# Graph attention on one core: the turns of the probabilities one by one between the output products of the chunk before

## The chip, the cores and the metric

One core of a Trainium2 chip. The metric is device time in microseconds from the kernel's start to its end; lower is better.

## The reference, cut to what matters

The kernel runs four layers one after the other on 1250 rows of 512 numbers: a graph attention, a gated feed-forward, a graph mean with a feed-forward, and a self-attention with a mixture of experts. The change is in the first:

```python
q = (x @ Wq + bq).reshape(n, H, OUT_DIM)      # n = 1250, H = 4, OUT_DIM = 512
k = (x @ Wk + bk).reshape(n, H, OUT_DIM)
v = (x @ Wv + bv).reshape(n, H, OUT_DIM)
alpha = jnp.einsum('ehc,ehc->eh', q[dst], k[src]) / np.sqrt(OUT_DIM)
amax = jax.ops.segment_max(alpha, dst, num_segments=n)
ex = jnp.exp(alpha - amax[dst])
denom = jax.ops.segment_sum(ex, dst, num_segments=n)
attn = ex / denom[dst]
agg = jax.ops.segment_sum(attn[:, :, None] * v[src], dst, num_segments=n).reshape(n, HC)
x_attn = agg + x @ Wskip + bskip
x_lin = x_attn @ Wlin + blin
...
```

## The kernel before

The attention over 21250 edges is computed densely: a matrix of edge counts, 1250 by 1250, is made in advance, and each head then computes all scores, masks those without an edge, and weights the exponentials by the counts. Products of weights that follow each other (Wq with Wk, Wv with Wlin) are folded in advance: `m` stands for the first and `g` for the second.

Each of the 4 heads has 5 chunks of 250 destination rows, and a chunk has two tiles of 125 rows (`s` is 0 or 1). All products of this layer are in three passes: each operand is kept as a rounded high half and a low half, and high by high, high by low, low by high are accumulated (`three_pass`, L127). So what leaves PSUM is evicted twice: ACT rounds it to the high half, then DVE subtracts that from the same bank to give the low half, and signals the bank as free.

For a chunk, PE does in this order:

- four `t_units`: the chunk's rows times `m`, 12 matmuls of 250 columns each, into two banks in turn (`unit`, banks 6 and 7), evicted to `t_hi`, `t_lo`;
- `y_unit(0)` of the chunk before (30 matmuls of 250 columns: probabilities times rows), then `scores(0)`, `y_unit(1)`, `y_unit(2)`, `scores(1)`, `y_unit(3)`. Units of y use the same two banks and are evicted to `yt_hi` and `yt_lo` (L1108 on ACT, L1188 on DVE);
- `turn(0)`: the ten pieces of the probabilities `prob` of tile 0, 125 by 125 each, are transposed on PE into three banks, in pieces of 4, 4 and 2 (`PIECES`), each piece with a signal `tp_done`; they are evicted to `pt_hi` (L1131 on ACT) and `pt_lo` (L1234 on DVE, `turn_lo`), which frees the piece's bank (`tp_free`);
- `out_units`: for each tile of the chunk before, 12 matmuls of 512 columns of `yt` by `g`, into the two unit banks again. A wait on `pp_free` ahead of them asks that all four y units are evicted. DVE adds each to `acc` (`add_out`, L1242);
- `turn(1)`: the same for tile 1.

While PE does so, DVE takes the maximum of a tile's scores, ACT the exponential, and DVE multiplies by the counts with the sum, and scales (`normalise_sum`, whose last step, L1228, signals `p_ready`). DVE's queue at a chunk's end is: the y unit's low half, `normalise_sum(1)`, `turn_lo(0)`, at the last chunk of a head the split of the next head's matrix (`split_lo`, L1172, behind ACT's L1102, which itself stands behind ACT's part of tile 0's turns), `add_out` twice, `turn_lo(1)`, and then the next chunk's t units. All queues are in program order and all waits are on semaphores, with values counted (`Tick`).

The first chunk of the first head has no chunk before it (`before is None`) and puts products of the skip path in these places. The outputs of the last chunk come at the end, from `last_outputs`, with no turns. In the last head DVE also normalises finished chunks.

Of the kernel before, what the change touches and what calls it, by code (L numbers as in the profile page):

```python
# [23 lines left out]
P = 125  # L24
NT = N // P
CH = 2 * P
NC = N // CH
KT = D // 128
# [64 lines left out]
class Core:  # L93
# [12 lines left out]
    def at(self, name, shape, dtype, kb):  # L106

        return self.nc.alloc_sbuf_tensor_at(name, shape, dtype, offset=self.bottom + int(kb * 1024))

    def sem(self, name):  # L110

        if name in self.credits:
            return self.credits[name]
        self.parts.append(self.nc.alloc_semaphore(name=name))
        return self.parts[-1]
# [7 lines left out]
    def bank(self, b):  # L123
        return self.psum[:, b, :]


def three_pass(nc, out, lhs, rhs, start, stop):  # L127

    (lh, ll), (rh, rl) = lhs, rhs
    nc.tensor.matmul(out, lh, rh, start=start, stop=False)  # L130
    nc.tensor.matmul(out, lh, rl, start=False, stop=False)  # L131
    return nc.tensor.matmul(out, ll, rh, start=False, stop=stop)  # L132
# [806 lines left out]
def graph_attention(core, g, w):  # L939
# [5 lines left out]
    nc, at, sem = core.nc, core.at, core.sem  # L945
# [3 lines left out]
    g_hi, g_lo = at("vl_hi", [128, KT, D], F32R, 128), at("vl_lo", [128, KT, D], F32R, 136)  # L949
# [7 lines left out]
    yt_hi, yt_lo = at("yt_hi", [128, KT, CH], F32R, 144), at("yt_lo", [128, KT, CH], F32R, 148)  # L957
    pt_hi, pt_lo = at("pt_hi", [P, NT, CH], F32R, R + 8), at("pt_lo", [P, NT, CH], F32R, R + 18)
    prob = at("prob", [P, 2, N], F32, R + 28)
# [7 lines left out]
    pp_done, pp_free, pp_hi = sem("pp_done"), sem("pp_free"), sem("pp_hi")  # L967
    s_done, s_free, m_ready, e_ready = sem("s_done"), sem("s_free"), sem("m_ready"), sem("e_ready")
    p_ready, tcol_ready = sem("p_ready"), sem("tcol_ready")
    tcol = at("t_col", [128, KT], F32, g.small + .5)  # L970
    tp_done, tp_hi, tp_free = sem("tp_done"), sem("tp_hi"), sem("tp_free")
# [10 lines left out]
    PIECES = [(0, 4), (4, 8), (8, 10)]  # L982
# [3 lines left out]
    def skip_bank(t):  # L986
        return core.bank(3 + t % 3)[0:P, :]

    def piece(q):
        j0, j1 = PIECES[q]  # L990
        return core.bank(3 + q)[0:P, 0:(j1 - j0) * P].rearrange("p (j n) -> p j n", n=P)

    def pipeline(eng, chunk, last_outputs, counts):

        chunk(0, 0, None)
        for h in range(HEADS - 1):
            chunk(h, 1, 0)  # L1000
            with eng.Fori(2, NC - 1) as c:
                for tick, per in counts:
                    tick.enter(c - 2, per)
                chunk(h, c, c - 1)
                for tick, per in counts:
                    tick.leave(NC - 3)
            chunk(h, NC - 1, NC - 2)
            chunk(h + 1, 0, NC - 1)
        for c in range(1, NC):
            chunk(HEADS - 1, c, c - 1)  # L1010
        last_outputs()

    with nc.Block() as block:
# [152 lines left out]
        def _(dve):  # L1166
# [17 lines left out]
            def unit_lo(dst_hi, dst_lo, n=D, bias=None):  # L1184
                _, b = unit()
                dve.wait_ge(pp_hi, hi.step())
                if bias is None:
                    ins = nc.vector.tensor_tensor(dst_lo, b[:, 0:n], f32(dst_hi), ALU.subtract)  # L1188
                else:
                    ins = nc.vector.scalar_tensor_tensor(dst_lo, b[:, 0:n], bias, f32(dst_hi), ALU.add, ALU.subtract)  # L1190
                ins.then_inc(pp_free, 1)
# [129 lines left out]
        @block.tensor  # L1321
        def _(pe):
            pp, tp, sub = Tick(), Tick(), Tick()

            def unit():
                v = pp.step()
                pe.wait_ge(pp_free, v)
                return bank(pp.n - 1)

            def skip(t):  # L1330
                if t >= 3:
                    pe.wait_ge(skip_added, t - 2)
                for k in range(KT):
                    pe.wait_ge(gs_lo, k + 1)
                    last = three_pass(nc, skip_bank(t), [a[:, k, t * P:(t + 1) * P] for a in (g.xt_hi, g.xt_lo)],
                                      [a[:, k, :] for a in (g_hi, g_lo)], k == 0, k == KT - 1)
                last.then_inc(skip_done, 1)

            def t_units(c):
                for m in range(KT):  # L1340
                    out = unit()
                    for k in range(KT):
                        last = three_pass(nc, out[:, 0:CH], [x[:, k, m * 128:(m + 1) * 128] for x in (m_hi, m_lo)],
                                          [x[:, k, bass.ds(CH * c, CH)] for x in (g.xt_hi, g.xt_lo)],
                                          k == 0, k == KT - 1)
                    last.then_inc(pp_done, 1)

            def scores(s, t_end):
                if s == 0:
                    pe.wait_ge(pp_free, t_end + 2)  # L1350
                pe.wait_ge(s_free, sub.step())
                for a, b in SPANS:
                    for k in range(KT):
                        last = three_pass(nc, score[:, a:b], [x[:, k, s * P:(s + 1) * P] for x in (t_hi, t_lo)],
                                          [x[:, k, a:b] for x in (g.xt_hi, g.xt_lo)], k == 0, k == KT - 1)
                last.then_inc(s_done, 1)

            def turn(s):
                v = tp.step()
                pe.wait_ge(p_ready, v)  # L1360
                pe.wait_ge(tp_free, 3 * v)
                for q, (j0, j1) in enumerate(PIECES):
                    for j in range(j0, j1):
                        last = nc.tensor.transpose(piece(q)[:, j - j0, :], prob[:, s, j * P:(j + 1) * P],
                                                   g.ident[0:P, 0:P])
                    last.then_inc(tp_done, 1)

            def y_unit(m):
                if m == 0:
                    pe.wait_ge(tp_free, 3 * (tp.base + tp.n) + 3)  # L1370
                out = unit()
                for j in range(NT):
                    last = three_pass(nc, out[:, 0:CH], [x[:, j, m * 128:(m + 1) * 128] for x in (g.xn_hi, g.xn_lo)],
                                      [x[:, j, :] for x in (pt_hi, pt_lo)], j == 0, j == NT - 1)
                last.then_inc(pp_done, 1)

            def out_units():
                pe.wait_ge(pp_free, pp.base + pp.n + 2)
                for s in range(2):
                    out = unit()  # L1380
                    for k in range(KT):
                        last = three_pass(nc, out[0:P, :], [x[:, k, s * P:(s + 1) * P] for x in (yt_hi, yt_lo)],
                                          [x[:, k, :] for x in (g_hi, g_lo)], k == 0, k == KT - 1)
                    last.then_inc(pp_done, 1)

            def chunk(h, c, before):
                def y(m):
                    if before is not None:
                        y_unit(m)
                    else:  # L1390
                        skip(AHEAD + m)

                if before is None:
                    for t in range(AHEAD):
                        skip(t)
                if isinstance(c, int) and c == 0:
                    pe.wait_ge(raw_free, 2 * h + 1)
                t_units(c)
                t_end = pp.base + pp.n
                y(0)  # L1400
                scores(0, t_end)
                y(1), y(2)
                scores(1, t_end)
                y(3)
                if before is None:
                    pe.wait_ge(skip_added, NT)
                turn(0)
                if before is not None:

                    pe.wait_ge(raw_free, 2 * h + (0 if isinstance(c, int) and c == 0 else 2))  # L1410
                    out_units()
                turn(1)

            def last_outputs():
                for m in range(KT):
                    y_unit(m)
                out_units()

            pipeline(pe, chunk, last_outputs, ((pp, 10), (tp, 2), (sub, 2)))


# [1682 lines left out]
```

## Time and profile before

| what | value |
|---|---|
| median of 3 runs | 2220.4 us (2218.78 to 2223.68) |
| span of the profiled execution | 2220.5 us; no other time is given for this execution |
| PE busy, matmuls | 2059.9 us, 93% |
| DVE busy | 1323.4 us, 60% |
| ACT busy | 836.3 us, 38% |
| POOL busy | 360.1 us, 16% |
| mean granted clock of PE | 0.969 |
| graph attention, the changed stage | from about 415 to 1229 us |

Engines: PE is TensorE's matmul, PEld its weight load, DVE VectorE, ACT ScalarE, POOL GpSimd. A row of the timeline gives start, duration, engine, line, operation, output and inputs; equal instructions that follow each other are merged, and then the duration reaches from the first one's start to the last one's end. Matmuls are pipelined, so a matmul's duration is longer than its distance to the next. In square brackets stands how long the engine was idle before, and what ended that. A granted clock of 1.00 is TensorE's full 2.4 GHz.

### The profile page before, as it was taken

Reading aid. Unit: us, or ns where it says so; the run is one execution under the profiler, and the core shown is the slowest. Engines: PE = TensorE matmul, PEld = TensorE weight load, DVE = VectorE, ACT = ScalarE, POOL = GpSimd, SP = SyncE. Lnnn points to the kernel's source line nnn. Section 1 sums busy time; section 2 is a strip of 40 time slices with the busy share of each in tenths; the row PEclk is TensorE's granted clock in tenths of the full one; section 3 lists DMA queues with packets and bytes.
Section 4 is the critical chain, followed back from the end, with each engine's and each line's share of the span. In section 5 each row is a group of like instructions: output and inputs, shape, how many; then the busy total and the mean of one; then the engine's idle time right before and its main releaser. Section 6 shows DMA issues by size and latency. Waiting matters only on the chain. (4 is left out here: it accounts for less than half of the span.)

```text
span 2220.5 us, 36706 instructions
## 1 busy us (share of the span) xinstructions
PE 2059.9 (93%) x13310; PEld 1806.2 (81%) x13310; DVE 1323.4 (60%) x2952; ACT 836.3 (38%) x1586; POOL 360.1 (16%) x308
## 2 busy tenths in 40 slices
PE   7998998999999999999999689999998999999586
PEld 5776667899999999999988569989878888888475
DVE  4574784443453454453678645556557878878766
ACT  3663993221221122122221312333336555555421
POOL 1000111000000000000000101111314453554243
PEclk9998999999999999999999889999998999999798
DMA  8760003122121211130101220201421021120542
GB/s 263 225 192 2 23 23 94 50 75 64 37 84 36 64 66 55 41 83 18 48 34 37 97 86 1 96 19 38 151 72 27 20 56 28 28 56 9 170 151 97
DMA packets 79516, 156.34 MB, mean 70 GB/s; under 512 B 7429, under 2 KB 22338, under 8 KB 77854
## 3 DMA queue, kind: packets, MB, share of 16 engines
q1 hardware_dynamic: 69802, 134.63, 20.1%
q0 software_dynamic: 4960, 11.49, 1.6%
q10 hardware_dynamic: 4616, 8.40, 1.1%
q8 instruction: 84, 1.38, 0.3%
q14 instruction: 54, 0.44, 0.1%
HBM read 104.17 MB, written 50.32 MB: 70 GB/s over the span
## 5 line engine op out<-in xcount | busy, mean ns | idle before, releaser
L130 PE MATMUL psum<-pt_hi,xn_hi 125*128 125x250 f32 x800 | 225.0, 281 | 3.3 <-DVE yt_lo L1188 1.6
L131 PE MATMUL psum<-pt_lo,xn_hi 125*128 125x250 f32 x800 | 223.8, 280 | 0.0
L132 PE MATMUL psum<-pt_hi,xn_lo 125*128 125x250 f32 x800 | 222.8, 278 | 0.0
L2412 POOL TENSOR_TENSOR mprob<-mprob,mrden 125x1250 f32<-125x1250 f32 x80 | 181.7, 2272 | 229.9 <-DVE mrden L2518 229.4
L1122 ACT ACTIVATE prob<-prob,nb 125x1250 f32<-125x1250 f32 x40 | 53.7, 1342 | 346.0 <-DVE nb L1215 346.0
L131 PE MATMUL psum<-xt_lo,t_hi 128*125 128x512 f32 (+1 forms) x480 | 170.1, 354 | 0.0
L132 PE MATMUL psum<-xt_hi,t_lo 128*125 128x512 f32 (+1 forms) x480 | 169.8, 354 | 0.0
L130 PE MATMUL psum<-xt_hi,t_hi 128*125 128x512 f32 (+1 forms) x480 | 169.1, 352 | 0.0
L2441 ACT ACTIVATE mprob<-psum,mbias 125x1250 f32<-125x1250 f32 x80 | 104.3, 1304 | 157.7 <-DVE mbias L2527 157.7
L130 PEld LDWEIGHTS psum<-pt_hi,xn_hi 125*128 125x128 f32 x800 | 151.2, 189 | 3.9 <-DVE yt_lo L1188 2.0
L2525 DVE TENSOR_REDUCE mmin<-psum 125x1 f32<-125x512 f32 (+1 forms) x240 | 127.1, 584 | 44.4 <-PE psum L2684 44.1
L131 PEld LDWEIGHTS psum<-pt_lo,xn_hi 125*128 125x128 f32 x800 | 152.1, 190 | 0.0
L132 PEld LDWEIGHTS psum<-pt_hi,xn_lo 125*128 125x128 f32 x800 | 151.8, 190 | 0.0
L704 PE MATMUL psum<-hot_src,hot_dst 125*125 125x512 bf16 (+1 forms) x624 | 131.8, 343 | 12.4 <-DVE hot_src L670 10.3
L2702 PE MATMUL psum<-ident,mprob 125*125 125x125 f32 x800 | 117.8, 292 | 21.7 <-DVE ptm_lo L2532 14.2
L2702 PEld LDWEIGHTS psum<-ident,mprob 125*125 125x125 f32 x800 | 100.1, 191 | 39.1 <-DVE ptm_lo L2532 24.8
L670 DVE TENSOR_SCALAR hot_src<-node_ids,src_f 125x1250 bf16<-125x1250 f16 x208 | 112.3, 555 | 32.3 <-PE psum L705 21.3
L2532 DVE TENSOR_TENSOR ptm_lo<-psum,ptm_hi 125x500 fp32r<-125x500 f32 (+1 forms) x240 | 126.4, 582 | 1.9 <-ACT ptm_hi L2447 1.9
L130 PE MATMUL psum<-ptm_hi,v_hi 125*128 125x250 f32 x400 | 114.8, 287 | 4.4 <-DVE ctx_lo L2538 4.4
L1209 DVE MEMSET mxc<- 125x1 f32 x40 | 2.4, 59 | 192.7 <-PE psum L132 192.7
L2684 PE MATMUL psum<-k_stack,q_chunk 128*125 128x512 f32 (+1 forms) x480 | 114.4, 375 | 2.9 <-PEq L120 2.9
L1089 POOL TENSOR_TENSOR fin_row<-fin_row 125x512 f32<-125x512 f32 x1 | 1.3, 1280 | 710.3 <-DMA gamma<-in_gamma 710.3
(503 smaller groups left out, 5854.7 us busy)
## 6 DMA issues: line engine op xcount, KB each, us to landing
slots_in<-slots_blank SPq DMA_DIRECT2D x12, 1282.5 KB, 9.2
cnt<-edge_counts SPq DMA_DIRECT2D x40, 305.2 KB
q_chunk<-q_store SPq DMA_DIRECT2D x40, 250.0 KB, 6.1
edge_attr<-in_attr SPq DMA_DIRECT2D x4, 1204.0 KB
slots_in<-slots_blank SPq DMA_DIRECT2D x3, 1539.0 KB, 16.0
moe_xg<-slots_in SPq DMA_DIRECT2D x17, 256.5 KB
raw_WvT<-in_WvT SPq DMA_DIRECT2D x4, 1024.0 KB, 6.0
raw_WskipT<-in_WskipT SPq DMA_DIRECT2D x4, 1024.0 KB, 11.8
```

The costliest lines, as they stand in the source:

```text
L130: nc.tensor.matmul(out, lh, rh, start=start, stop=False)
L131: nc.tensor.matmul(out, lh, rl, start=False, stop=False)
L132: return nc.tensor.matmul(out, ll, rh, start=False, stop=stop)
L670: nc.vector.tensor_scalar(hot_src[:, a, :], g.node_ids[0:P, :], g.src_f[:, bass.ds(GROUP * j + a, 1)], None, ALU.is_equal).then_inc(ready, 1)
L704: nc.tensor.matmul(acc[:, a:b], hot_dst[:, s, 0:P], hot_src[:, s, a:b], start=first, stop=False)
L1122: nc.scalar.activation(prob[:, s, :], prob[:, s, :], ACT.Exp, bias=nb[:, s:s + 1], scale=scale).then_inc(e_ready, 1)
L2412: nc.gpsimd.tensor_tensor(prob[:, n % 4, :], prob[:, n % 4, :], rden[:, n % 4:n % 4 + 1].broadcast_to([P, N]), ALU.mult).then_inc(p_ready, 1)
L2441: nc.scalar.activation(prob[:, n % 4, :], score[:, 0:N], ACT.Exp, bias=bias[:, n % 4:n % 4 + 1], scale=-1.0, accum_out=den[:, n % 4:n % 4 ...
L2525: last = nc.vector.tensor_reduce(low[:, s, q:q + 1], score[:, a:b], AX.X, ALU.min)
L2532: nc.vector.tensor_tensor(pt_part(n, 1, j0, j1), piece(q), f32(pt_part(n, 0, j0, j1)), ALU.subtract).then_inc(tp_free, 1)
L2684: last = nc.tensor.matmul(score[:, a:b], qs[:, half, n // 2, cols], g.k_stack[:, n // 2, a:b], start=half == 0, stop=half == 1)
L2702: last = nc.tensor.transpose(piece(q)[:, j - j0, :], prob[:, n % 4, j * P:(j + 1) * P], g.ident[0:P, 0:P])
```

## The change

The ten turns of a tile no longer form a block of their own. A new function, `out_units_and_turns`, issues the 12 matmuls of an output unit and puts one turn behind each of the second to the eleventh. Tile 0's turns go between the products of the first output unit, tile 1's between those of the second. The wait for the tile's probabilities (`turn_ready`) stands behind the unit's first product. The wait for free banks is split: each piece waits for its own bank (`turn_one`), where before a turn began when all three were free. The order of the three passes within a product group stays. The wait on `pp_free` for the evicted y units stands at the head of the new function, so it is now ahead of all turns. The first chunk keeps its turns in blocks, and the other engines' programs are as they were.

```diff
--- before.py
+++ after.py
@@ -1355,15 +1355,22 @@
                                           [x[:, k, a:b] for x in (g.xt_hi, g.xt_lo)], k == 0, k == KT - 1)
                 last.then_inc(s_done, 1)
 
+            def turn_one(s, j):
+                q = next(i for i, (j0, j1) in enumerate(PIECES) if j0 <= j < j1)
+                j0, j1 = PIECES[q]
+                if j == j0:
+                    pe.wait_ge(tp_free, 3 * (tp.base + tp.n - 1) + q + 1)
+                last = nc.tensor.transpose(piece(q)[:, j - j0, :], prob[:, s, j * P:(j + 1) * P], g.ident[0:P, 0:P])
+                if j == j1 - 1:
+                    last.then_inc(tp_done, 1)
+
+            def turn_ready():
+                pe.wait_ge(p_ready, tp.step())
+
             def turn(s):
-                v = tp.step()
-                pe.wait_ge(p_ready, v)
-                pe.wait_ge(tp_free, 3 * v)
-                for q, (j0, j1) in enumerate(PIECES):
-                    for j in range(j0, j1):
-                        last = nc.tensor.transpose(piece(q)[:, j - j0, :], prob[:, s, j * P:(j + 1) * P],
-                                                   g.ident[0:P, 0:P])
-                    last.then_inc(tp_done, 1)
+                turn_ready()
+                for j in range(NT):
+                    turn_one(s, j)
 
             def y_unit(m):
                 if m == 0:
@@ -1382,6 +1389,24 @@
                         last = three_pass(nc, out[0:P, :], [x[:, k, s * P:(s + 1) * P] for x in (yt_hi, yt_lo)],
                                           [x[:, k, :] for x in (g_hi, g_lo)], k == 0, k == KT - 1)
                     last.then_inc(pp_done, 1)
+
+            def out_units_and_turns():
+                pe.wait_ge(pp_free, pp.base + pp.n + 2)
+                for s in range(2):
+                    out = unit()
+                    for k in range(KT):
+                        cols = slice(s * P, (s + 1) * P)
+                        passes = ((yt_hi, g_hi), (yt_hi, g_lo), (yt_lo, g_hi))
+                        for i, (left, right) in enumerate(passes):
+                            n = 3 * k + i
+                            last = nc.tensor.matmul(out[0:P, :], left[:, k, cols], right[:, k, :], start=n == 0,
+                                                    stop=n == 3 * KT - 1)
+                            if n == 3 * KT - 1:
+                                last.then_inc(pp_done, 1)
+                            if n == 0:
+                                turn_ready()
+                            if 1 <= n <= NT:
+                                turn_one(s, n - 1)
 
             def chunk(h, c, before):
                 def y(m):
@@ -1404,12 +1429,12 @@
                 y(3)
                 if before is None:
                     pe.wait_ge(skip_added, NT)
-                turn(0)
-                if before is not None:
-
+                if before is None:
+                    turn(0)
+                    turn(1)
+                else:
                     pe.wait_ge(raw_free, 2 * h + (0 if isinstance(c, int) and c == 0 else 2))
-                    out_units()
-                turn(1)
+                    out_units_and_turns()
 
             def last_outputs():
                 for m in range(KT):
```

## Rows read from the trace of the kernel before

**Rows 1.** Busy time by stage: us, PE, PEld, DVE, ACT, POOL busy, PEclk, DMA.
```profile
414.00:1229.00 815.00, 806.84 (x5529) 737.76 (x5528) 408.02 (x925) 181.91 (x319) 13.60 (x6) 1.00 0.16 52
1229.00:2220.50 991.50, 885.23 (x5874) 789.59 (x5874) 669.05 (x1636) 415.43 (x816) 311.22 (x239) 0.95 0.23 67
```

**Rows 2.** PE's grouped lines, 414 to 1229: busy, mean ns, idle before, releaser.
```profile
L130 PE MATMUL psum<-vl_hi,yt_hi 128*125 128x512 f32 x160 | 65.0, 406 | 0.9 <-DVE yt_lo L1188 0.9
...
L1364 PE MATMUL psum<-ident,prob 125*125 125x125 f32 x380 | 47.8, 273 | 1.1 <-DVE pt_lo L1234 1.1
```

**Rows 3.** Timeline of PE in one chunk: start us, us, engine, line, operation.
```profile
611.73 0.28 PE L132 MATMUL psum<-pt_hi,xn_lo 125*128 125x250 f32 x1
...
612.08 0.27 PE L132 MATMUL psum<-pt_hi,xn_lo 125*128 125x250 f32 x1
612.19 1.25 PE L1364 MATMUL psum<-ident,prob 125*125 125x125 f32 x10
613.32 0.47 PE L130 MATMUL psum<-vl_hi,yt_hi 128*125 128x512 f32 x1
613.62 0.39 PE L131 MATMUL psum<-vl_lo,yt_hi 128*125 128x512 f32 x1
...
618.75 0.40 PE L132 MATMUL psum<-vl_hi,yt_lo 128*125 128x512 f32 x1
618.98 1.25 PE L1364 MATMUL psum<-ident,prob 125*125 125x125 f32 x10
...
620.19 0.28 PE L131 MATMUL psum<-xt_lo,qk_hi 128*128 128x250 f32 x1
```

**Rows 4.** Timeline of DVE in the same chunk.
```profile
612.80 0.42 DVE L1188 TENSOR_TENSOR yt_lo<-psum,yt_hi 128x250 fp32r<-128x250 f32 x1 [1.83 <-ACT yt_hi L1108]
...
615.20 0.87 DVE L1228 TENSOR_SCALAR prob<-prob,rden 125x1250 f32<-125x1250 f32 x1
615.99 1.58 DVE L1234 TENSOR_TENSOR pt_lo<-psum,pt_hi 125x500 fp32r<-125x500 f32 x3
...
619.18 0.69 DVE L1242 TENSOR_TENSOR acc<-acc,psum 125x512 f32<-125x512 f32 x1 [1.02 <-PE psum L132]
```

**Rows 5.** Timeline of PE behind the last chunk.
```profile
1219.99 0.27 PE L132 MATMUL psum<-pt_hi,xn_lo 125*128 125x250 f32 x1
1221.18 0.49 PE L130 MATMUL psum<-vl_hi,yt_hi 128*125 128x512 f32 x1 [0.92 <-DVE yt_lo L1188]
```

**Rows 6.** Timeline of PE's weight loads behind the second block of turns.
```profile
619.97 0.19 PEld L130 LDWEIGHTS psum<-xt_hi,qk_hi 128*128 128x128 f32 x1
620.08 0.19 PEld L131 LDWEIGHTS psum<-xt_lo,qk_hi 128*128 128x128 f32 x1
```

**Rows 7.** Timelines of PE, ACT and DVE at a change of head.
```profile
571.76 0.39 PE L131 MATMUL psum<-vl_lo,yt_hi 128*125 128x512 f32 x1
...
577.12 1.25 PE L1364 MATMUL psum<-ident,prob 125*125 125x125 f32 x10
578.65 0.35 PE L130 MATMUL psum<-xt_hi,qk_hi 128*128 128x250 f32 x1 [0.28 <-DVE acc L1242]
...
572.17 1.93 ACT L1102 ACTIVATE qk_hi<-raw 128x2048 fp32r<-128x2048 f32 x1
...
575.63 2.28 DVE L1172 TENSOR_TENSOR qk_lo<-raw,qk_hi 128x2048 fp32r<-128x2048 f32 x1
577.83 1.28 DVE L1242 TENSOR_TENSOR acc<-acc,psum 125x512 f32<-125x512 f32 x2
...
580.90 0.48 DVE L1190 SCALAR_TENSOR_TENSOR t_lo<-psum,t_cols,t_hi 128x250 fp32r<-128x250 f32 x1 [0.30 <-ACT t_hi L1110]
```

**Rows 8.** Timelines of DVE and PE in the last two chunks.
```profile
1154.19 2.84 DVE L1228 TENSOR_SCALAR prob<-prob,rden 125x1250 f32<-125x1250 f32 x1
...
1158.68 1.32 PE L1364 MATMUL psum<-ident,prob 125*125 125x125 f32 x10 [0.55 <-DVE pt_lo L1234]
...
1203.77 0.38 PE L130 MATMUL psum<-pt_hi,xn_hi 125*128 125x250 f32 x1 [1.65 <-DVE pt_lo L1234]
```

## The prediction

> **What bounds the kernel now.** I read the page's shares first: PE is busy for 93% of the span (the table above), too coarse to place an edit. The busy times by stage come next: from 414 to 1229 us, where the graph attention runs, PE is busy for 806.84 of 815.00 us at a granted clock of 1.00, its full 2.4 GHz [rows 1]. So in this stage the end is set by what PE's queue holds plus every gap in it, one for one. The grouped lines of the stage put 0.9 us of idle time in all ahead of the output products and 1.1 us ahead of the turns [rows 2]. DVE is busy for half of it (408 us), ACT for 182: both matter only where PE waits for them.
>
> Then one chunk of the timeline, PE alone [rows 3]. A matmul is best timed from start to start. Output products: second at 613.62, last (22 later) at 618.75: 0.233 us each. Turns: ten in 1.25 us of which the last takes 0.27, so 0.109 each. Matmuls of 250 columns: three steps from 611.73 to 612.08, 0.117 each. The reader is to see what stands at 612.19: the ten turns of tile 0, exactly between the last y product and the first output product. And at that moment [rows 4] ACT has rounded the last y unit, and DVE makes its low half from 612.80 for 0.42 us, to 613.22; the first output product, whose operand that is, starts at 613.32. **The ten turns lie in the shadow of an eviction.** They end at 613.28, just as the operand comes.
>
> The same wait without turns in front of it stands in the trace once: the outputs after the last chunk. Last y product 1219.99, first output product 1221.18, and PE idle 0.92 us for yt_lo [rows 5]. That is 1.19 us from start to start, where 612.08 to 613.32 is 1.24 with ten turns inside.
>
> **The change, part by part.** Nothing is added or taken from PE's work: 24 output products and 20 turns a chunk, as before, in 19 chunks (380 turns [rows 2]; the first chunk keeps its blocks). No DMA is moved. What moves is turn(0): it goes behind the wait for pp_free, which stays at the head of the outputs.
>
> 1. *The lost cover.* yt_lo comes from the y product's end, by an ACT and a DVE instruction that the change doesn't touch, so the second output product stays at 613.62. Behind it now come 22 further products and 20 turns instead of 22 and 10. Last output product: 613.62 + 22 x 0.233 + 20 x 0.109 = 620.93; the second t product then at 621.28, against 620.19 [rows 3]: +1.09 us, which is ten turns. In 18 chunks 19.6 us; the last chunk is summed under 5.
>
> 2. *A turn between two products.* What a turn costs there no row shows whole, but both of its seams do. Product then turn: 618.75 to 618.98, 0.23, a plain product's step. Turn then product of another kind: the last turn starts at about 619.96, the second matmul behind it at 620.19, so 0.23 for the two steps, 0.11 + 0.12. The loads tell why: the load for the matmul behind a turn starts with that turn (619.97), and the next load starts 0.11 later (620.08) [rows 6]; one load is ahead, never two. So a product covers the turn's load, as it may be hoped, but a turn is too short to cover the product's. I take 0.109, as in a block. Ends: no less than 0.057 (125 columns at a product's 512 in 0.233), which gives back 380 x 0.052 = 19.8 us; at most 0.11 more at each seam, 380 x 0.11 = 42 us, if passing between the two kinds drained PE as 613.32 to 613.62 might be read (I put that 0.30 down to yt_lo).
>
> The Trainium skill ("TensorE: Matmul & The Clock Gate", "Back-to-back issue gap") gives N/2.4 + 2.5 ns, here 55 ns, for a matmul's step and, under "LDWEIGHTS", P/1.2, here 104 ns, for its load. By the second the trace's 0.109 is a load's pace, which agrees; by the first alone a turn between products would cost 55 ns.
>
> 3. *t products of the next chunk.* add_out(1) follows the last product by 0.43 (618.75 to 619.18 [rows 3, 4]): 621.36. turn_lo(1) stands behind it on DVE; an add gives DVE on after 0.60 (two take 1.28 [rows 7], one 0.69), turn_lo after 1.50 (1.58 with the end of its last [rows 4]), then t_lo(0) takes 0.48 [rows 7]: 621.36 + 0.60 + 1.50 + 0.48 = 623.94, and 0.07 for the signal. The third t unit wants its bank at 621.16 + 23 x 0.117 = 623.85. It waits 0.16 in 15 chunks: 2.4 us. Bounds 0 and 0.3. The add is now late because the last product is.
>
> 4. *Change of head*, three times. turn_lo(0), the split of the next matrix and both adds stand in front of the t unit's bank; PE already waits there, until 578.65, where its turns from 577.12 end at about 578.1 [rows 7]: 0.5. The last turn of tile 0 now starts at 571.76 + 9 x 0.342 + 0.23 = 575.07; ACT rounds it by about 575.7 and splits for 1.93 (to 577.6), DVE splits for 2.28 and adds to about 580.6, and PE starts about 580.75, where its queue would let it at 571.76 + 22 x 0.233 + 2.18 + 0.23 = 579.3. The wait grows from 0.5 to 1.45: 0.9 x 3 = 2.7 us.
>
> 5. *The tile's probabilities, needed earlier.* The wait for p_ready of tile 1 moves from behind 24 products to behind 13 and ten turns: to 613.62 + 11 x 0.233 + 10 x 0.109 = 617.3. They are ready at 615.20 + 0.87 = 616.07 [rows 4], 1.2 us early, so in 16 chunks free. In the last three L1228 takes over 2 us, 2.84 in the chunk of 1154 [rows 8], and PE waits already. There: ready at 1154.19 + 2.84 = 1157.03; wanted some 0.8 earlier; then turn_lo's first piece frees its bank only at about 1157.7, for 1157.3 wanted: in all about 1.1 of waiting against 0.7 before (the turns' start at 1158.68, of which the row calls 0.55 idle). So +0.4 for it and +0.4 likewise for the one before. The last chunk has 1.09 and 0.4 as well, and behind it y comes at once, with no t units to cover turn_lo(1): 0.43 + 0.60 + 1.50 + 0.1, or 2.6 from the last product, where y now starts 1.9 after the last turn (1203.77 [rows 8], the last turn at about 1201.9). With a product's 0.2 off, +0.5: 2.0 for this chunk.
>
> 6. *Waits split by piece*: a bank's release is asked for piece by piece. Nothing is waited for there in 16 chunks, as PE is slower than the evictions; free.
>
> Sum: 19.6 + 2.4 + 2.7 + 0.8 + 2.0 = 27.5 us. On the profiled span of 2220.5 us, 2248.0; the median of the runs shown is 2220.4, so the same number stands for it: **2248 us, 1.2% slower**.
>
> **The rivals.**
> *A, a turn between products costs 0.057.* Its load hides under the product before it; for the product's own load to hide as well, loads would have to run two ahead. The Trainium skill ("TensorE: Matmul & The Clock Gate", "Step-by-step: what each phase is for") says that the queue can pull weight loads ahead of running matmuls, which would be its way. Against it: every load in the rows starts with the matmul before its own. 27.5 - 19.8 = 7.7: 2228.
>
> *B, each change of kind drains PE.* +42: 2290. For it the 0.30 at 613.32; against it 0.23 at 618.75 and at 619.96.
>
> *C, faster: the turn rides free.* Between two products it would add nothing, its columns too streaming while the next load runs. Then 380 x 0.109 = 41.4 us go, 27.5 come: 2206. It decides from a price below 0.037 a turn (0.109 less 27.5/380). Nothing in the rows has two matmuls in PE at full rate at once.
>
> *D, the clock.* PE now idles 0.9 us in each of 19 chunks. The granted clock stayed at 1.00 in this stage over a gap of 1.65 us [rows 1, 8]; behind 1229, where gaps are common, the mean is 0.95. At 0.95 the stage's 807 us would be some 42 longer: 2290 with the rest.
>
> *E, no change*: it would need the wait of 1 to vanish, though the order of waits forbids it, or a price just at 0.037.
>
> **How the numbers follow.** Forecast case 0.78, its own range 2242 to 2256 (step 3 from 0 to 0.3 us a chunk, steps 4 and 5 at half to double, without the last chunk's 1.1 of turns). A 0.10, B 0.05, C 0.02, D 0.03, E 0.02. The range reaches part of the way to A and B, 2236 to 2260, and leaves 0.19 outside. Within 0.2% (4.4 us), about what this measurement can tell from no change: E and the upper edge of C, 0.03. Faster 0.03, slower 0.94.
>
> **What the changed profile would show.** Step 1: the grouped line of L130 on vl_hi, yt_hi with 17 to 18 us of idle ahead of it (0.9 now), released by DVE yt_lo, and 1.2 us from the last y product to the first output product in each chunk. Step 2: in the timeline of PE a product and its turn at 0.34 for the pair; 0.29 would be A, 0.45 B. Step 3: third t unit idle by 0.1 to 0.2, released by DVE t_lo. Step 4: L130 on qk_hi idle 1.2 or so at each new head, on DVE acc. Step 5: no idle at the turns until the last three chunks. The graph attention ends 27 us later, the stages behind it take as long as now. The prediction fails if a turn between products isn't a load's 0.109, or if the y unit's eviction isn't what the first output product waits for.

## The result

The changed kernel takes 2246.3 us (median of 4 runs, 2243.21 to 2247.62) against 2221.1 us (4 runs, 2218.78 to 2223.68): ratio 1.0107, 95% interval 1.0093 to 1.0121, so 1.1% slower. Forecast were 2248 us and 1.2%. The profiled executions differ by 24.7 us of span (2245.2 against 2220.5). Here and below medians and ratios leave out two executions that ran at a lower granted clock (one of e4, 2569.3 us at 0.74, and one of e8, 2391.9 us at 0.939).

First the busy time by stage of the changed kernel, which answers to [rows 1] (the attention now ends 28 us later, so its window is longer by that):

```profile
414.00:1257.00 843.00, 812.41 (x5520) 739.53 (x5519) 407.69 (x926) 189.65 (x318) 14.64 (x7) 1.00 0.16 50
1257.00:2245.20 988.20, 882.85 (x5874) 787.80 (x5874) 667.63 (x1636) 415.04 (x816) 310.27 (x239) 0.96 0.23 67
```

PE is as busy as before, 812 us for 807, at the same clock of 1.00; 28 us were added to the window and only 5.6 of them are busy. PE's grouped lines in that window say where the rest stands (columns as in [rows 2]):

```profile
L1402 PE MATMUL psum<-vl_hi,yt_hi 128*125 128x512 f32 x152 | 70.7, 465 | 18.5 <-issue 12.6 <-DVE yt_lo L1188 6.0
L1402 PE MATMUL psum<-vl_lo,yt_hi 128*125 128x512 f32 x152 | 69.5, 458 | 1.2 <-DVE prob L1228 1.2
L130 PE MATMUL psum<-xt_hi,qk_hi 128*128 128x250 f32 x201 | 57.3, 285 | 3.6 <-DVE acc L1242 3.5
```

The first of these lines, which holds the first product of each unit, has 18.5 us of idle time ahead of it, where [rows 2] had 0.9. Part of it is put down to DVE's yt_lo and part to "issue", which here only means that the profile found no event to name: in all 19 chunks the first output product starts 1.24 to 1.27 us behind the last y product, and 0.10 to 0.13 us behind the end of the same eviction. In the timeline of PE in the chunk of [rows 3], now 4.6 us later:

```profile
616.66 0.27 PE L132 MATMUL psum<-pt_hi,xn_lo 125*128 125x250 f32 x1
617.90 0.47 PE L1402 MATMUL psum<-vl_hi,yt_hi 128*125 128x512 f32 x1 [0.97 <-issue]
618.21 0.40 PE L1402 MATMUL psum<-vl_lo,yt_hi 128*125 128x512 f32 x1
618.44 0.27 PE L1363 MATMUL psum<-ident,prob 125*125 125x125 f32 x1
618.47 0.47 PE L1402 MATMUL psum<-vl_hi,yt_lo 128*125 128x512 f32 x1
618.78 0.27 PE L1363 MATMUL psum<-ident,prob 125*125 125x125 f32 x1
...
625.45 0.47 PE L1402 MATMUL psum<-vl_hi,yt_lo 128*125 128x512 f32 x1
625.76 0.28 PE L130 MATMUL psum<-xt_hi,qk_hi 128*128 128x250 f32 x1
625.87 0.28 PE L131 MATMUL psum<-xt_lo,qk_hi 128*128 128x250 f32 x1
```

and of DVE beside it:

```profile
617.38 0.42 DVE L1188 TENSOR_TENSOR yt_lo<-psum,yt_hi 128x250 fp32r<-128x250 f32 x1 [1.83 <-ACT yt_hi L1108]
...
619.78 0.87 DVE L1228 TENSOR_SCALAR prob<-prob,rden 125x1250 f32<-125x1250 f32 x1
...
625.96 0.69 DVE L1242 TENSOR_TENSOR acc<-acc,psum 125x512 f32<-125x512 f32 x1 [2.60 <-PE psum L1402]
626.57 1.58 DVE L1234 TENSOR_TENSOR pt_lo<-psum,pt_hi 125x500 fp32r<-125x500 f32 x3
628.06 0.47 DVE L1190 SCALAR_TENSOR_TENSOR t_lo<-psum,t_cols,t_hi 128x250 fp32r<-128x250 f32 x1
```

The last y product starts at 616.66, the first output product at 617.90, 1.24 us behind it as before, and nothing stands between them now. DVE's yt_lo (617.38, 0.42 us) ends at 617.80. From there all is dense: turn to turn 0.34 us (618.44, 618.78), and the second t product comes at 625.87, 9.21 us behind the last y product, where [rows 3] show 620.19 - 612.08 = 8.11.

### The profile page after: what moved, and what is told of

It reads as the page before. It is cut to its first block and busy times, and to the rows that moved or that the text cites. A ratio compares the mean times of both kernels' runs of the same rounds, so it can differ in the third digit from the quotient of the medians.

```text
span 2245.2 us, 36698 instructions
## 1 busy us (share of the span) xinstructions
PE 2064.9 (92%) x13310; PEld 1806.5 (80%) x13310; DVE 1321.8 (59%) x2952; ACT 844.1 (38%) x1586; POOL 360.5 (16%) x308
## 3 DMA queue, kind: packets, MB, share of 16 engines
q1 hardware_dynamic: 69802, 134.63, 19.8%
```

## The experiments

Two theories. **Mine**: the ten turns of tile 0 lost the eviction that covered them, and a turn costs the same between products as in a block. **S**: the alternation of turns and products is itself what costs. After the first four runs a question of its own was left: why does a turn cost 0.109 us wherever it stands. Times are medians, each beside the kernel before on the same chip.

### e1: only the wait moved

```diff
                 if before is None:
                     pe.wait_ge(skip_added, NT)
+                else:
+                    pe.wait_ge(pp_free, pp.base + pp.n + 2)
                 turn(0)
```

> The kernel before with one line more: the wait for all four evicted y units stands ahead of the first block of turns instead of behind it. Nothing is interleaved. Lost cover (my theory): 1.2 us from the last y product to the first turn, ten turns of 1.09 us uncovered in 19 chunks, 20.7 us, less some 1.5 us at the three changes of head and 1.6 us in the last head, where PE waits now and would then come later: 2239, between 2236 and 2243. Rival S, that alternating turns and products is what costs: 2221, no change.

2238.1 us against 2222.1, ratio 1.0069 (1.0054 to 1.0084). PE's timeline at a chunk's end (the last chunk of a head):

```profile
575.38 0.27 PE L132 MATMUL psum<-pt_hi,xn_lo 125*128 125x250 f32 x1
576.58 1.35 PE L1364 MATMUL psum<-ident,prob 125*125 125x125 f32 x10 [0.92 <-DVE yt_lo L1188]
577.69 0.48 PE L130 MATMUL psum<-vl_hi,yt_hi 128*125 128x512 f32 x1
```

Nothing is interleaved in this kernel, and the gap of 0.92 us with ten uncovered turns behind it is there. From the last y product to the last t product of the next chunk each plain chunk takes 1.07 to 1.09 us more than before. **S is refuted as the cause of the bulk.** This one line makes 16 of the change's 25 us. The rest comes from what the interleaving delays: chunk by chunk, the attention of the changed kernel's trace is longer than e1's by 4.2 us at the three changes of head, 2.8 us in the other 13 chunks (at their third t units, step 3 below) and 3.8 us in the last three (10.8 in all; step 6 below takes 1.3 off in the first chunk).

### e2: tile 0's turns as a block ahead of the wait, tile 1's between products

```diff
             def out_units_and_turns():
+                turn(0)
                 pe.wait_ge(pp_free, pp.base + pp.n + 2)
...
-                            if n == 0:
+                            if n == 0 and s == 1:
                                 turn_ready()
-                            if 1 <= n <= NT:
+                            if 1 <= n <= NT and s == 1:
                                 turn_one(s, n - 1)
```

> The changed kernel with tile 0's turns again as a block ahead of the wait for the y units; only tile 1's stand between products. Theory: the 1.09 us a chunk come back (first output product 1.24 us behind the last y product with ten turns between), but tile 1's turns are now wanted at about the time when DVE has scaled the probabilities and before it has freed the first piece: 0.4 us of waiting on DVE pt_lo a chunk, 0.2 at the third t unit, 1.5 in the last three chunks: 2233, between 2228 and 2237. Rival S gives half of the change's loss, 2234, but with no waits at the turns and more than 0.35 us for a product with its turn; the trace tells them apart.

2230.1 us, ratio 1.0026 (1.0012 to 1.0041). With the cover back, 16 us of the loss are gone, though half of the interleaving stands. What is left is waiting, as foreseen, but smaller in the plain chunks (0.2 us, not 0.4) at tile 1's first turn:

```profile
616.64 0.39 PE L1403 MATMUL psum<-vl_hi,yt_hi 128*125 128x512 f32 x1
616.87 0.40 PE L1403 MATMUL psum<-vl_lo,yt_hi 128*125 128x512 f32 x1
617.19 0.37 PE L1363 MATMUL psum<-ident,prob 125*125 125x125 f32 x1
617.32 0.47 PE L1403 MATMUL psum<-vl_hi,yt_lo 128*125 128x512 f32 x1
617.63 0.27 PE L1363 MATMUL psum<-ident,prob 125*125 125x125 f32 x1
617.66 0.47 PE L1403 MATMUL psum<-vl_hi,yt_hi 128*125 128x512 f32 x1
```

617.19 is 0.32 us behind the product before it instead of 0.23, and the turn's own record is 0.10 longer than the next one's, 0.2 in all; after that a product and its turn take 0.34 again (617.32, 617.66). In the last three chunks the loss is 1.5, 1.6 and 3.6 us.

### e3: all turns between products, the y unit waited for late

The last y unit is the last quarter (`k` = 3) of what an output product sums over. So the first nine products don't need it.

```diff
-                pe.wait_ge(pp_free, pp.base + pp.n + 2)
+                last_y = pp.base + pp.n + 2
...
                             n = 3 * k + i
+                            if s == 0 and n == 3 * (KT - 1):
+                                pe.wait_ge(pp_free, last_y)
```

> The changed kernel, all turns between products, but the wait for the last y unit stands only ahead of the three output products that read it (the tenth to twelfth of the first unit). Theory: no gap behind the y products (0.11 us instead of 1.24), and in its place some 0.4 us a chunk at tile 1's first turn on DVE pt_lo, over 2 us in the last three, 1 us more at the three changes of head: 2236, between 2230 and 2240, at least 6 us under the changed kernel. Rival S: the alternation stays as it is, so 2246 less 2 at most.

2237.8 us, ratio 1.0075 (1.0061 to 1.009): 8 us under the changed kernel's 2246; expected were 2236 and at least 6 us less. PE's timeline:

```profile
611.91 0.27 PE L132 MATMUL psum<-pt_hi,xn_lo 125*128 125x250 f32 x1
612.03 0.39 PE L1404 MATMUL psum<-vl_hi,yt_hi 128*125 128x512 f32 x1
...
616.15 0.40 PE L1404 MATMUL psum<-vl_lo,yt_hi 128*125 128x512 f32 x1
616.55 0.37 PE L1363 MATMUL psum<-ident,prob 125*125 125x125 f32 x1
616.68 0.47 PE L1404 MATMUL psum<-vl_hi,yt_lo 128*125 128x512 f32 x1
```

The gap behind y is closed (611.91 to 612.03) and a gap opens at tile 1's first turn: 0.40 us from 616.15 where a product takes 0.23, and 0.1 in the turn itself. DVE scales that tile's probabilities at 615.04 + 0.87 and frees the first piece's bank 0.67 later, at about 616.6. So the order of the change has a second lateness behind its first: without the gap, tile 1's turns are wanted before their data is there.

### e4: turns in blocks, late wait, banks waited for by piece

```diff
                 pe.wait_ge(p_ready, v)
-                pe.wait_ge(tp_free, 3 * v)
                 for q, (j0, j1) in enumerate(PIECES):
+                    pe.wait_ge(tp_free, 3 * (tp.base + tp.n - 1) + q + 1)
...
             def out_units():
-                pe.wait_ge(pp_free, pp.base + pp.n + 2)
+                last_y = pp.base + pp.n + 2
...
+                        if s == 0 and k == KT - 1:
+                            pe.wait_ge(pp_free, last_y)
```

> The kernel before, turns in blocks, with the change's piece by piece wait for banks and with the wait for the last y unit ahead of the three products that read it. Theory: 0.12 us a chunk between the first turns and the first product (2.2 us), 1.2 us in the first chunk, where the second block starts on its first piece's bank, 1.6 us in the last three: 5 us faster than before, 2216, between 2214 and 2219. Rival: the gap of 0.12 us is PE changing kind and stays, then 2218 to 2219.

2217.3 us against 2222.1, ratio 0.998 (0.9971 to 0.9988), within the range expected. From the last y product to the first output product it is now 1.12 us, and from the last turn to it 0.03, the step also seen ahead of every t product:

```profile
609.80 0.27 PE L132 MATMUL psum<-pt_hi,xn_lo 125*128 125x250 f32 x1
609.91 1.25 PE L1364 MATMUL psum<-ident,prob 125*125 125x125 f32 x10
610.92 0.47 PE L130 MATMUL psum<-vl_hi,yt_hi 128*125 128x512 f32 x1
611.24 0.39 PE L131 MATMUL psum<-vl_lo,yt_hi 128*125 128x512 f32 x1
```

The plain chunks become 0.11 to 0.18 us shorter each and the last three 0.3 to 0.5; at the three changes of head nothing is gained, since PE waits there anyway. The rival (the 0.12 is PE changing kind) is refuted: the kinds still change, and the gap is gone.

### e5b and e6b: turns that load 64 columns instead of 125

In both, 7 of 10 turns transpose only the first 64 columns of their piece; the other columns of those pieces aren't computed. e5b is the changed kernel, e6b the kernel before.

```diff
+                m = P if j == j0 else 64
-                last = nc.tensor.transpose(piece(q)[:, j - j0, :], prob[:, s, j * P:(j + 1) * P], g.ident[0:P, 0:P])
+                last = nc.tensor.transpose(piece(q)[0:m, j - j0, :], prob[:, s, j * P:j * P + m], g.ident[0:P, 0:P])
```

> The changed kernel in which 7 of each 10 turns take only 64 of the 125 columns of their piece (the rest isn't transposed, so the numbers of the attention are wrong). Their weight load is half as long, the columns that stream are the same 125. Theory (a turn costs what the load of the product behind it takes): nothing changes, a product with its turn stays at 0.34 us, 2246. Rival (the turn's own load is what costs): 0.05 us less for each of 266 narrow turns, 14 us, 2232.

> The kernel before with the same 7 of 10 turns narrow, in blocks (the rest of those pieces isn't transposed). Theory: in a block the next turn's load sets the pace, so narrow turns follow each other at about 0.06 instead of 0.109 us: a block of ten takes 0.75 instead of 1.09. Tile 0's block lies under the eviction and gives nothing, tile 1's gives 0.35 us in 19 chunks: 2215, between 2212 and 2219. Rival (0.109 is a turn's own passage, whatever it loads): no change, 2222.

e5b takes 2247.3 us (ratio 1.0114, 1.0098 to 1.0129), no change from the changed kernel, and a product with its turn stays at 0.34 us. e6b takes 2219.9 us against 2221.7, ratio 0.9993 (0.9982 to 1.0004), no measurable change, **where my theory wanted 2215**. Tile 1's block in e6b, first in PE's timeline:

```profile
619.61 1.24 PE L1365 MATMUL psum<-ident,prob 125*125 125x125 f32 x10
```

then the same block by the turns' line (min, median and max of a record in ns):

```profile
L1365 PE MATMUL psum<-ident,prob x10: 268/270/273, 619.6 to 620.6; 125*64 125x125 f32 x7, 125*125 125x125 f32 x3
L1365 PEld LDWEIGHTS psum<-ident,prob x9: 110/112/188, 619.6 to 620.5; 125*64 125x64 f32 x7, 125*125 125x125 f32 x2
```

The loads did become shorter (110 ns of record against 188), but ten turns take 1.24 us where they took 1.25. Start to start, a step is 0.106 to 0.107 us where the next turn loads 64 columns and 0.109 where it loads 125. So in a block the pace isn't set by the load alone, as the prediction had it: a turn's own 125 columns need about 0.106 us. This also takes the force out of e5b: its unchanged time was foreseen by the theory, but would be the same if only the turn's own columns counted.

### e8 to e10: turns of 64 rows

Here 7 of 10 turns take only 64 of the tile's 125 rows, so that 64 columns stream through PE, over 64 rows of it; the other rows of those pieces aren't turned. e8 is the changed kernel with 125 columns loaded, e9 the kernel before with the same, e10 the kernel before with 64 columns loaded as well.

```diff
+                        m = P if j == j0 else 64
-                        last = nc.tensor.transpose(piece(q)[:, j - j0, :], prob[:, s, j * P:(j + 1) * P],
-                                                   g.ident[0:P, 0:P])
+                        last = nc.tensor.transpose(piece(q)[0:m, j - j0, 0:m], prob[0:m, s, j * P:j * P + m],
+                                                   g.ident[0:m, 0:m])
```

(in e8 and e9 `piece(q)[:, j - j0, 0:m]` and `prob[0:m, s, j * P:(j + 1) * P]`).

> The changed kernel in which 7 of each 10 turns take only 64 of the tile's 125 rows: all 125 columns are loaded, but only 64 stream (the other rows aren't turned, so the attention's numbers are wrong). The run with short loads has shown that a turn needs 0.106 us for its own 125 columns. If the load of the product behind the turn needs as long (theory, kept in this half), a product with a short turn stays at 0.34 us and the time at 2246. If only the turn's own columns counted (rival A of the prediction in new form), a pair falls to 0.29, 0.05 us for each of 266 turns, 13 us: 2233.

> The kernel before with the same short turns in blocks: 125 columns loaded, 64 streamed in 7 of 10. Theory: the next turn's load binds as well and takes 0.105, so a block of ten stays at 1.07 to 1.09 us and the time at 2222. If columns that stream were the only bound, 0.055 a short turn, a block of 0.71, and tile 1's blocks give 0.36 us 19 times, 7 us: 2215.

> The kernel before, blocks, with 7 of 10 turns of 64 rows and 64 columns: both load and stream are half. Theory (two bounds of equal size, load and stream, and the longer one sets the pace): now the pace of short turns falls to 0.055 to 0.06 us where the next one is short too (5 of 10 steps), 0.11 otherwise: a block of about 0.83 instead of 1.09, tile 1's blocks give 0.26 us 19 times, 5 us: 2217. Rival (a floor of 0.106 for any turn, whatever it loads and streams): no change, 2222.

All three are slower, which none of the theories had: e9 2253.4 us (ratio 1.0145, 1.0128 to 1.0163), e10 2237.7 (1.0075, 1.0058 to 1.0092), e8 2366.1 (1.0646, 1.0577 to 1.0716; its executions lie between 2348.5 and 2382.1). As whole runs they say nothing on the question, for a cost of their own covers it: passing between a turn of 125 rows and one of 64. The step into the first short turn of a block is 0.20 us and the step from the next long turn to the short one behind it 0.30, in both kernels, where e6b has 0.11. A block of ten takes 2.05 us in e9 and 1.61 in e10, where it was 1.25:

```profile
620.20 2.05 PE L1365 MATMUL psum<-ident,prob 125*125 125x125 f32 x10
```

```profile
615.90 1.61 PE L1365 MATMUL psum<-ident,prob 125*125 125x125 f32 x10
```

The step between the second and the third short turn of a piece, though, stands apart from that (the one between the first and the second doesn't: 0.16 us in e9, 0.08 in e10). Such a pair alone, of e9 and then of e10 (its duration less one record of 0.27 and 0.22 us is the step):

```profile
620.56 0.38 PE L1365 MATMUL psum<-ident,prob 64*125 64x64 f32 x2
```

```profile
616.18 0.27 PE L1365 MATMUL psum<-ident,prob 64*64 64x64 f32 x2
```

64 streamed and 125 loaded: 0.38 - 0.27 = 0.11 us. 64 and 64: 0.27 - 0.22 = 0.05, or 0.055 to 0.056 start to start. And e6b's 125 streamed and 64 loaded: 0.106. So there are two bounds on a turn's step, its own columns and the next load, and at 125 by 125 they are nearly equal; only when both are cut does the step fall. These are steps of one execution each (two in each of 38 blocks, all within 0.001 us of each other), not a time of a run. And since a short turn has both fewer columns and fewer rows, the runs don't tell which of the two makes its step shorter. e8 gives no verdict on a pair: the granted clock in its attention is 0.93, which alone disturbs the comparison.

### e7b: e4 with the split of the next matrix earlier

```diff
                 units[1](), units[2]()
+                if split:
+                    split_in(2 * h + 3, m_hi)
...
                 turn_hi(0)
-                if split:
-                    split_in(2 * h + 3, m_hi)
...
                 mask(1, it)
+                if split:
+                    split_lo(2 * h + 3, m_hi, m_lo)
...
                 turn_lo(0)
-                if split:
-                    split_lo(2 * h + 3, m_hi, m_lo)
```

> e4 with the split of the next head's matrix earlier in a head's last chunk: ACT's part behind its third y unit and DVE's behind the second mask, both where these engines idle. Theory: the wait at the first t unit of a new head goes (0.64 us from where the queue would let it, three times): 2 us less than e4, 2215.5, between 2213 and 2217.5. Rival: the 4 us of splitting delay the second tile's maximum or exponential in that chunk, and the time is e4's 2217.7 or more.

2214.9 us against 2221.7, ratio 0.9967 (0.9955 to 0.9979), the fastest version of this study. At the change of head of [rows 7] the t product now follows the last turn at once:

```profile
576.85 1.25 PE L1364 MATMUL psum<-ident,prob 125*125 125x125 f32 x10
577.86 0.36 PE L130 MATMUL psum<-xt_hi,qk_hi 128*128 128x250 f32 x1
```

## Why the prediction was right, point by point

**Step 1, the lost cover**: right. +1.10 us from the last y product to the second t product (9.21 against 8.11), forecast 1.09; in 18 chunks 19.8 us. e1 makes this term by itself with one line. It comes to 17.1 us there and not 19.8, because at the changes of head and in the last three chunks PE already waits in the kernel before, and the later arrival fills part of that wait.

**Step 2, a turn between products**: the number was right, 0.34 us for a pair (618.44 to 618.78, and all through the block), the reason half wrong. I put 0.109 down to weight loads, one ahead and no more, and took 0.057, a product's pace of columns, as the turn's own need. e6b contradicts that: with the load about halved the step stays at 0.106. A turn's column takes twice a product's (0.106/125 = 0.85 ns against 0.233/512 = 0.455). So the lower end of the range, and rivals A and C with it, had no ground from either side: neither a load that runs further ahead nor a covered load could have made a turn cheaper. That the load of what follows is a bound too is shown only for turns behind turns (e9's step of 0.11), not for a product behind a turn. One reading of the rows was wrong besides: the 0.30 from 613.32 to 613.62, put down to yt_lo, stands in e4 too (610.92 to 611.24), where nothing waits for yt_lo. With the 0.03 ahead of it, it is the step of the last turn and that of the first product, 0.34 together, and so no sign of a drain for B.

The Trainium skill ("TensorE: Matmul & The Clock Gate", "Back-to-back issue gap" and "LDWEIGHTS") gives 55 ns for a step of 125 columns alone and 104 ns for their load. The second agrees with e9 (0.11 us with 125 columns loaded and 64 streamed). The first doesn't hold for these turns: e6b measures 0.106 us with 64 loaded, and the measurement decides. The page calls its first figure the gap of an isolated matmul; the 81 ns that it gives for 128 columns in a stream of loads and matmuls is under e6b's step too.

**Step 3, the third t unit**: the sum was right by luck, 2.5 us in 13 chunks for 2.4 in 15. In plain chunks the wait is 0.10 us (forecast 0.16), in the six chunks that run in a loop (`Fori`, the third and fourth of the first three heads) 0.2 to 0.6. One such wait, PE at the third t unit of the chunk of 625.76, against 0.12 for a step:

```profile
628.45 0.28 PE L132 MATMUL psum<-xt_hi,qk_lo 128*128 128x250 f32 x1
628.58 0.38 PE L130 MATMUL psum<-xt_hi,qk_hi 128*128 128x250 f32 x1
628.80 0.28 PE L131 MATMUL psum<-xt_lo,qk_hi 128*128 128x250 f32 x1
```

The longer waits in the loops stood in the trace of before, unread: the forecast took `add_out` 0.43 us behind the last product from a plain chunk, and in the six loop chunks of before it comes 0.55 to 0.91 behind. The changed kernel adds 0.08 to both (0.51 plain, 0.63 to 0.99 in the loops), and the third t unit waits longer by what the add is later. What makes the add late there was not tried.

**Step 4, the change of head**: right, 0.87 us three times, forecast 0.9. DVE's split and adds, then PE:

```profile
580.22 2.29 DVE L1172 TENSOR_TENSOR qk_lo<-raw,qk_hi 128x2048 fp32r<-128x2048 f32 x1 [1.28 <-ACT qk_hi L1102]
582.42 1.28 DVE L1242 TENSOR_TENSOR acc<-acc,psum 125x512 f32<-125x512 f32 x2
...
583.25 0.35 PE L130 MATMUL psum<-xt_hi,qk_hi 128*128 128x250 f32 x1 [1.17 <-DVE acc L1242]
```

The t product waits 1.17 us for the bank that `add_out` frees, where [rows 7] show 0.28.

**Step 5, the probabilities needed earlier**: right in place, 0.4 and 0.6 us in the two chunks (forecast 0.4 each; here 0.15 and 0.1 of it stand at the third t unit) and 2.05 in the last (2.0). L1228 took 3.08 us in the chunk that had 2.84 in [rows 8]. DVE and PE there, then PE behind the last turns:

```profile
1177.19 3.08 DVE L1228 TENSOR_SCALAR prob<-prob,rden 125x1250 f32<-125x1250 f32 x1
...
1180.33 0.50 PE L1402 MATMUL psum<-vl_lo,yt_hi 128*125 128x512 f32 x1 [0.67 <-DVE prob L1228]
...
1230.57 0.38 PE L130 MATMUL psum<-pt_hi,xn_hi 125*128 125x250 f32 x1 [2.28 <-DVE pt_lo L1234]
```

**Step 6, waits by piece**: called free, and it was a gain that I missed, since I looked only at the 19 chunks with outputs. In the first chunk the second block of turns has no products before it and PE waits for banks; it now starts on the first piece's. In the trace of before the block starts at 409.20 after 3.10 us of idle, 4.46 us behind the first block's start at 404.74; now:

```profile
405.16 1.35 PE L1363 MATMUL psum<-ident,prob 125*125 125x125 f32 x10 [0.85 <-DVE acc L1178]
408.70 2.12 PE L1363 MATMUL psum<-ident,prob 125*125 125x125 f32 x10 [2.19 <-DVE pt_lo L1234]
410.49 0.56 PE L130 MATMUL psum<-xt_hi,qk_hi 128*128 128x250 f32 x1
```

3.54 us behind. The y products behind the first chunk end 1.3 us earlier than in the trace of before. It is not chance: in the four other traces whose turns wait for all banks at once the distance of the blocks is 4.45 to 4.46, in the five others that wait by piece 3.54 to 3.55.

Sum by the trace, last y product of the first chunk with outputs to the first y product behind the last: 18 x 1.10 + 2.5 + 2.6 + 1.0 + 2.05 = 28.0 us (forecast 27.5), less 1.3 in the first chunk. From the first y product behind the last chunk (1203.77, now 1230.57) to the end the changed kernel is 2.1 us shorter, with a granted clock of 0.96 for 0.95; nothing there was changed, and I take it for chance between two executions. The traces bear that out: with the same program this stretch takes 1016.7 us in the trace of before, 1014.6 in the changed kernel's, 1017.2 in e1's and 1013.4 in e2's. 28.0 - 1.3 - 2.1 = 24.6, and the spans differ by 24.7.

**The rivals.** B is refuted by the pair of 0.34 and by e1, A and C by the same pair, D by the clock of 1.00 in the attention over 19 gaps, E by the result.

## What to carry to other kernels

Before a block of work is spread out for density, look at what it hides: a short block between a producer's last matmul and its first consumer may cost nothing where it stands and its full length elsewhere. Ask of a wait which instructions really read what it guards; moved from the head of the unit to its last three products, it gave back 8 of the 25 us lost (e3), and in blocks, with the waits by piece, made the kernel faster than before (e4). And one lateness can hide another: e3 removed the first and met the second, so price the next one before the first is taken away.

## What the runs showed of the hardware

- A turn (a transpose of fp32 data) of 125 columns needs 0.106 us for itself (e6b), 0.85 ns a column, where a product of the same kernel has 0.455 (512 columns in 0.233 us). That is about as long as the step takes with 125 columns loaded and 64 streamed (0.11, e9). Only with both cut to 64 does the step fall, to 0.055 us (e10).
- Passing between turns that use 125 rows and 64 rows costs: ten turns take 2.05 us instead of 1.25 when 7 use 64 rows, and 19 chunks with it 31 us (e9). That it is the rows is argued, not tried by itself: columns loaded change in e6b, and columns streamed between product and turn in the changed kernel, without such a cost.
- The same mix between products (e8) takes 2366 us, and in its profiled execution (2391.9 us) the granted clock from 450 to 1200 us is 0.93, where every other kernel here has 1.00. Why the clock falls there was not tried.
